# Moving an output product, sharing a division, writing a mask on another engine, and reordering the seam between two stages

## The reference, cut to what matters

```python
x = x + _L1_xattn_ref(_layernorm(x), ctx_1024, ctx_1024, mask_ik0, ...)    # 16 heads of 8, keys: 77
x = x + _L1_ffn_ref(_layernorm(x), ...)
x = x + _L2_xattn_ref(_layernorm(x), ctx_1024, ctx_1024, mask_fk1, ...)    # the same shape
x = x + _L2_ffn_ref(_layernorm(x), ...)      # 6 layers: windowed attention, then a gated FFN
x = x + _L3_xattn_ref(ctx_1024, _layernorm(x), mask_bk0, ...)              # 16 heads of 64, keys: 77 + 512
x = x + _L3_ffn_ref(x, ...)

def _L2_ffn_ref(...):                        # its last step, per layer
    xn = (x - mu) / jnp.sqrt(var + 1e-05) * g + bln
    a, gate = jnp.split(xn @ W1 + b1, 2, -1)
    return a * jax.nn.gelu(gate, approximate=False) @ W2 + b2

def _L3_xattn_ref(x, latents, mask, g1, b1, g2, b2, Wq, Wkv, Wout):
    xn, ln_lat = layer_norm(x, g1, b1), layer_norm(latents, g2, b2)
    q = ln_lat @ Wq
    k, v = jnp.split(jnp.concatenate([xn, ln_lat], axis=1) @ Wkv, 2, axis=-1)
    weight = jnp.einsum('bhld,bhnd->bhln', q * scale, k * scale)           # 512 x 589 per head
    weight = jnp.where(full_mask[:, None, None, :], weight, neg)           # only context keys are masked
    out = jnp.einsum('bhln,bhnd->bhld', softmax(weight), v)
    return out @ Wout
```

## Time and profile before

| | us |
|---|---|
| runs: median of 3 (lowest to highest) | 1956.83 (1955.41 to 1961.53) |
| the profiled execution, its own time | 1947.39 |
| its span, first to last instruction | 1945.5 |
| PE busy | 1621.7 (83%), mean granted clock 0.923 |
| DVE busy | 1255.0 (65%) |
| ACT busy | 968.0 (50%) |
| POOL busy | 761.1 (39%) |
| first attention, about | 230 to 301 |
| second attention, about | 484 to 555 |
| stack, about | 555 to 1480 |
| latents, about | 1490 to 1818 |

### The profile page before, as it was taken

One profiled execution on the slowest core, in us unless ns is written; L12 is line 12 of the kernel. 1 busy time (PEld: TensorE's weight loads), 2 busy tenths in 40 slices (PEclk: granted clock), 3 DMA queues, 4 the chain that ended last, 5 costly groups with the idle time before them and its releaser, 6 DMA issues.

```text
span 1945.5 us, 42200 instructions
## 1 busy us (share of the span) xinstructions
PE 1621.7 (83%) x17249; PEld 1097.3 (56%) x17249; DVE 1255.0 (65%) x2361; ACT 968.0 (50%) x1729; POOL 761.1 (39%) x1082
## 2 busy tenths in 40 slices
PE   3005576999767899989999889999987999999999
PEld 1002254676545666656666656666663677667576
DVE  6847684212866788868888778888853666666311
ACT  1034133332235567656666566666654666666332
POOL 0000020100247666766776657766740333334000
PEclk7556798899888999999999999999998999999999
DMA  3000002010033343433433343343311000000111
GB/s 108 20 4 0 3 1 62 22 33 14 1 113 98 98 117 102 124 81 105 118 103 102 101 102 101 117 109 89 96 35 43 2 1 1 1 2 1 33 33 33
DMA packets 73661, 113.33 MB, mean 58 GB/s; under 512 B 15942, under 2 KB 36012, under 8 KB 73438
## 3 DMA queue, kind: packets, MB, share of 16 engines
q1 hardware_dynamic: 72654, 110.40, 20.6%
q10 hardware_dynamic: 816, 0.24, 0.1%
HBM read 83.95 MB, written 27.50 MB: 57 GB/s over the span
## 4 chain that ended last, share of the span: by engine, by line
PE 60%; DVE 27%; issue 6%; ACT 4%; DVEq 1%; DMA 1%; POOL 0%; ACTq 0%; POOLq 0%; SPq 0%
PE PS L1385 7%; PE PS L1115 6%; PE PS L1106 6%; PE PS L2089 4%; PE PS L2043 3%; PE PS L1634 3%; PE PS L2068 3%; DVE st_t L1428 3%; DVE st_ss L1433 3%; PE PS L1514 2%; DVE st_r L1420 2%; PE PS L1493 2%; PE PS L1586 2%; PE PS L1733 2%; DVE al_hist L459 2%
## 5 line engine op out<-in xcount | busy, mean ns | idle before, releaser
L1462 POOL TENSOR_TENSOR st_r<-st_r,st_t 128x512 f32<-128x512 f32 x192 | 243.6, 1274 | 205.8 <-DVE st_t L1428 205.8
L1385 PE MATMUL PS<-st_wqkv,st_xs 128*128 128x512 f32 x576 | 304.8, 614 | 12.5 <-DVE st_t L1428 8.0
L2174 POOL TENSOR_SCALAR la_p<-la_p,la_rden 128x589 f32<-128x589 f32 x64 | 112.7, 1761 | 245.8 <-DVE la_rden L2193 245.8
L1479 POOL TENSOR_TENSOR st_r<-st_r,st_gy 128x512 f32<-128x512 f32 x192 | 195.1, 1047 | 3.8
L1420 DVE TENSOR_TENSOR st_r<-PS,st_rot 128x512 f32<-128x512 f32 x192 | 129.3, 673 | 99.0 <-ACT st_sqh L1404 98.4
L2187 DVE TENSOR_REDUCE la_nmx<-PS 128x1 f32<-128x589 f32 x128 | 92.7, 766 | 91.8 <-PE PS L2051 91.8
L2149 ACT ACTIVATE la_p<-PS,la_nmx 128x589 f32<-128x589 f32 x128 | 95.0, 747 | 106.6 <-DVE la_nmx L2187 106.6
L1174 ACT ACTIVATE m_h<-PS 128x512 f32<-128x512 f32 x128 | 76.1, 597 | 140.8 <-PE PS L1106 140.8
L1404 ACT ACTIVATE st_sqh<-PS 128x512 f32<-128x512 f32 x192 | 114.4, 596 | 57.4 <-PE PS L1385 56.3
L1199 DVE SCALAR_TENSOR_TENSOR m_y<-PS,m_g,m_y 128x128 f32<-128x128 f32 x112 | 31.5, 345 | 161.0 <-PE PS L1115 161.0
L1428 DVE TENSOR_TENSOR st_t<-PS,st_rot 128x512 f32<-128x512 f32 x192 | 130.6, 680 | 0.0
(11 more groups left out here) (313 smaller groups left out, 3487.4 us busy)
## 6 DMA issues: line engine op xcount, KB each, us to landing
st_v_out<-st_v SPq DMA_DIRECT2D x48, 512.0 KB, 2.6
st_vv<-st_v_out SPq DMA_DIRECT2D x96, 256.0 KB, 4.2
st_vv<-st_v_out SPq DMA_DIRECT2D x96, 192.0 KB, 4.5
st_wqkv<-in_st_wqkv SPq DMA_DIRECT2D x18, 512.0 KB, 5.7
m_w<-in_m_w SPq DMA_DIRECT2D x32, 256.0 KB, 3.1
st_vv<-st_v_out SPq DMA_DIRECT2D x72, 64.0 KB, 1.9
st_wo<-in_st_wo SPq DMA_DIRECT2D x6, 512.0 KB
st_w<-in_st_w SPq DMA_DIRECT2D x6, 341.0 KB
```

Source lines behind the costliest of these rows:

```text
L1385: pe.matmul(PS[:, 2 + m % 2, :], self.xs[:, b, P * t:P * t + P], self.wqkv[:, l % 2, k, 512 * half:512 * half + 512], start=True, stop=Tru ...
L1462: pool.tensor_tensor(r, r, self.t2[:, c % 2, :], ALU.add).then_inc(self.added, 1)
L1479: pool.tensor_tensor(r, r, y[:, 8 * c:8 * c + 8].unsqueeze(2).broadcast_to([P, 8, D2]), ALU.mult)\
L2174: pool.tensor_scalar(self.p[:, v % 2, 0, :], self.p[:, v % 2, 0, :], self.rden[:, v % 4, 0:1], None, ALU.mult).then_inc(self.scaled0, 1)
```

## The change

It has four parts.

1. **Attentions.** PE issues the output product of b=0 behind the scores of tile 6 (new `pe_out`, in step t=6) and no longer behind the mix of tile 3. ACT's copy to `l_o` now stands ahead of the exponential of that step. The division of the last tile is split (new `divide`): POOL takes heads 0 to 7, DVE heads 8 to 15, and PE's transposes wait for both.
2. **Stack, last unit.** The residual `xn` is added in `dve_xf`, for u=10 and u=11. The three chunks of u=11 use banks (6,7), (4,5), (0,1), so that no chunk waits for the one ahead of it, and `pe_down` waits chunk by chunk. Two table loads of ACT at the end are left out (the extra `ACT.Exp` ones).
3. **Seam.** The mean of b=0 is made right behind `pe_centre` of u=11, and its centring behind the last gate. The context pieces of latents (`ctx_pe`, `ctx_dve`) run ahead of `pe_down`. K and Q of b=0 start when b=0 is normed. V is made after them and waited for only in step v=1. The weights' transfers are issued when the stack's last projection is done.
4. **Latents.** The two mask products are gone. ACT writes the mask (128x77, bf16 in SBUF) into the PSUM columns of the context keys (`act_mask`), ahead of the scores, and the context product adds to it. The writes of v+1 stand in ACT's queue behind the copy L2162 of step v and ahead of the scaling L2168. The mask is prepared on 128 partitions.

```diff
                 pool.wait_ge(self.rden_ready, self.past["rden_ready"] + t + 1)
-                s = self.s[:, t % 3, 0:HK].rearrange("p (h k) -> p h k", h=H)
-                pool.tensor_tensor(s, s, self.rden[:, t % 2, :].unsqueeze(2).broadcast_to([P, H, KC]), ALU.mult)\
-                    .then_inc(self.probs, 1)
+                self.divide(pool, t, 0, H if t < NT - 1 else H // 2).then_inc(self.probs, 1)
+
+        def divide(self, eng, t, h0, h1):
+
+            s = self.s[:, t % 3, 0:HK].rearrange("p (h k) -> p h k", h=H)[:, h0:h1, :]
+            return eng.tensor_tensor(s, s, self.rden[:, t % 2, h0:h1].unsqueeze(2).broadcast_to([P, h1 - h0, KC]),
+                                     ALU.mult)
...
                                        kb[:, b, h0:h0 + nh, :].rearrange("p h k -> p (h k)"), start=True, stop=True)
                     mm.then_inc(self.scores, 1)
+                if t == NT // B + 2:
+                    self.pe_out(pe, 0)
                 if t >= 2:
                     u = t - 2
...
-                            pe.wait_ge(self.scores_read, self.past["scores_read"] + NT)
-                        pe.matmul(PS[:, 7 - 7 * b, :], self.wqo[:, 1, :], self.o[:, b, :], start=True, stop=True)\
-                          .then_inc(self.out_prod, 1)
+            pe.wait_ge(self.scores_read, self.past["scores_read"] + NT)
+            self.pe_out(pe, 1)
+
+        def pe_out(self, pe, b):
+
+            pe.wait_ge(self.o_ready, self.past["o_ready"] + b + 1)
+            pe.matmul(PS[:, 7 - 7 * b, :], self.wqo[:, 1, :], self.o[:, b, :], start=True, stop=True)\
+              .then_inc(self.out_prod, 1)
 
         def act(self, act):
...
                                        PS[:, 3 + g, 0:P * (c1 - c0)], ACT.Copy).then_inc(self.pT_ready, 1)
+                if t >= 2 and j == NT // B - 1:
+                    act.wait_ge(self.mixed, self.past["mixed"] + u + 1)
+                    act.activation(self.o[:, b, :], PS[:, 6, :], ACT.Copy).then_inc(self.o_ready, 1)
                 if t < NT:
                     act.wait_ge(self.centred, self.past["centred"] + t + 1)
                     s = self.s[:, t % 3, 0:HK]
                     act.activation(s, s, ACT.Exp).then_inc(self.exps, 1)
-                if t >= 2 and j == NT // B - 1:
-                    act.wait_ge(self.mixed, self.past["mixed"] + u + 1)
-                    act.activation(self.o[:, b, :], PS[:, 6, :], ACT.Copy).then_inc(self.o_ready, 1)
 
         def dve(self, dve):
...
                        .then_inc(self.centred, 1)
+            dve.wait_ge(self.rden_ready, self.past["rden_ready"] + NT)
...
+            latents.sp(sp)
 
...
+            if u // B == DEPTH - 1:
+
+                b = u % B
+                dve.wait_ge(self.xf_ready, u + 1)
+                order.link(dve, dve.tensor_tensor(x[:, b, :], x[:, b, :], xn[:, b, :], ALU.add))
...
+
+        def up_banks(self, u, j):
+            return ((6, 7), (4, 5), (0, 1))[j] if u == self.LAST else (6, 7)
+
         def pe_up(self, pe, u, j):
             l, (a, w) = u // B, self.CHUNKS[j]
+            gate, value = self.up_banks(u, j)
             if j == 0:
                 pe.wait_ge(self.ffn_in, u + 1)
                 pe.wait_ge(self.xu_ready, min(4 * u + 5, self.N))
-            else:
+            elif u < self.LAST:
                 pe.wait_ge(self.act_ready, 3 * u + j)
-            pe.matmul(PS[0:w, 6, :], self.w1[:, l % 2, FFI + a:FFI + a + w], self.xfn[:, :], start=True, stop=True)\
+            pe.matmul(PS[0:w, gate, :], self.w1[:, l % 2, FFI + a:FFI + a + w], self.xfn[:, :], start=True, stop=True)\
               .then_inc(self.up, 1)
-            pe.matmul(PS[0:w, 7, :], self.w1[:, l % 2, a:a + w], self.xfn[:, :], start=True, stop=True)\
+            pe.matmul(PS[0:w, value, :], self.w1[:, l % 2, a:a + w], self.xfn[:, :], start=True, stop=True)\
               .then_inc(self.up, 1)
 
         def act_gelu(self, act, u, j):
...
 
         def pe_down(self, pe, u):
             l = u // B
-            pe.wait_ge(self.act_ready, 3 * u + 3)
             for j, (a, w) in enumerate(self.CHUNKS):
+                if u == self.LAST or j == 0:
+                    pe.wait_ge(self.act_ready, 3 * u + (j + 1 if u == self.LAST else 3))
                 mm = pe.matmul(PS[:, 6, :], self.w2[0:w, l % 2, j, :], self.hid[0:w, j, :], start=(j == 0), stop=(j == 2))
             mm.then_inc(self.down, 1)
 
+        X_READY = 10
+
         def dve_down(self, dve, u):
             l, b = u // B, u % B
...
             dve.wait_ge(self.down, u + 1)
             dve.scalar_tensor_tensor(x[:, b, :], PS[:, 6, :], self.sv[:, l % 2, 2:3], x[:, b, :], ALU.add, ALU.add)\
-               .then_inc(self.down_added, 1)
-            dve.wait_ge(self.down_added, u + 1)
-            if u + B < B * DEPTH:
+               .then_inc(x_ready if final else self.down_added, 1)
+            if not final:
+                dve.wait_ge(self.down_added, u + 1)
                 self.shift(dve, b, self.xs[:, b, :], self.xs_ready)
 
...
                     self.pe_centre(pe, norm_of)
+                if norm_of == self.LAST:
...
                     self.pe_proj(pe, T + 2, 5)
+                if end_of == self.LAST:
+                    pe.wait_ge(self.act_ready, 3 * self.LAST + 1)
...
                     self.dve_gate(dve, end_of, 2)
-            for b in range(B):
-                dve.wait_ge(self.down_added, B * DEPTH)
-                dve.tensor_tensor(x[:, b, :], x[:, b, :], xn[:, b, :], ALU.add).then_inc(x_ready, 1)
+                if end_of == self.LAST:
...
 
         K0, K1, Q0, Q1, V0, V1, KCTX, VCTX = range(8)
         DVE_PIECES, ACT_PIECES = (K0, K1, KCTX, VCTX), (Q0, Q1, V0, V1)
-        FIRST_BANK = tuple(range(8))
+        FIRST_BANK = (0, 1, 2, 3, 6, 5, 7, 7)
+        FIRST = (KCTX, VCTX, K0, Q0, K1, Q1, V0, V1)
...
+        def ctx_pe(self, pe):
+
+            pe.wait_ge(align.cn_ready, 2)
+            pe.wait_ge(self.wc_in, self.c("wc_in", 16))
+            for k in (self.KCTX, self.VCTX):
+                self.pe_piece(pe, 0, k)
...
             for e in (1, 0):
-                pe.matmul(span[e][:, S:], q[e], self.k[rows[e], a, b, S:], start=True, stop=False,
-                          skip_group_check=True)
-            for e in (1, 0):
-                one = slice(D2 * e, D2 * e + 1)
-                pe.matmul(span[e][:, S:], oneb[one, :], mnegb[one, KC * b:KC * b + KC],
-                          start=False, stop=True, skip_group_check=True).then_inc(self.scores, 1)
+                pe.wait_ge(self.masked, 2 * v + 2 - e)
+                pe.matmul(span[e][:, S:], q[e], self.k[rows[e], a, b, S:], start=False, stop=True,
+                          skip_group_check=True).then_inc(self.scores, 1)
...
         def pe(self, pe):
-            norm.wait(pe, "pe")
-            pe.wait_ge(align.cn_ready, 2)
-            pe.wait_ge(self.wc_in, 16)
-            for k in range(self.PIECES):
-                self.pe_piece(pe, 0, k)
-            for k in range(self.PIECES):
+            for b, pieces in enumerate(((self.K0, self.Q0), (self.K1, self.Q1))):
+                norm.wait(pe, "pe", b + 1)
+                for k in pieces:
+                    self.pe_piece(pe, 0, k)
+            pe.wait_ge(*self.took(0, self.VCTX))
+            self.pe_piece(pe, 0, self.V0)
+            self.pe_piece(pe, 0, self.V1)
+            for k in (self.K0, self.Q0, self.K1, self.Q1, self.KCTX):
                 pe.wait_ge(*self.took(0, k))
             pe.wait_ge(self.w_in, self.c("w_in", 32))
             for v in range(self.STEPS):
                 self.pe_scores(pe, v)
+                if v == 1:
+                    for k in (self.V0, self.V1):
+                        pe.wait_ge(*self.took(0, k))
                 if v:
                     self.pe_turn(pe, v - 1)
...
             for k in self.ACT_PIECES:
                 self.act_piece(act, 0, k)
+                if k == self.Q1:
+                    act.wait_ge(*self.took(0, self.Q1))
+                    act.wait_ge(*self.took(0, self.K1))
+                    self.act_mask(act, 0)
...
+                if v + 1 < self.STEPS:
+                    self.act_mask(act, v + 1)
                 if v < self.STEPS:
                     self.act_scale(act, v)
+
+        def act_mask(self, act, v):
+
+            b = self.tile(v)[1]
+            if v:
+                act.wait_ge(self.exps, self.c("exps", 2 * v))
+            for e in (1, 0):
+                act.activation(self.span(e)[:, S:], mnegb[:, KC * b:KC * b + KC], ACT.Copy).then_inc(self.masked, 1)
```

130 lines of the change are left out of this document (73 added, 57 removed).

## The result

The changed kernel takes 1930.70 us, the median of 4 runs (1927.56 to 1934.96), against 1956.12 before: a ratio of 0.9865, with a 95% interval of 0.9835 to 0.9894. The gain of the medians is 25.4 us, and the interval reaches from 21 to 32; the forecast was 29.0. In a second comparison the same two kernels gave a ratio of 0.9856 (0.9834 to 0.9878), 24 to 33 us. Over the ten runs of both the changed kernel's median is 1930.7.

What follows compares the result with a forecast made beforehand. DVE was taken to bound the attentions, a chain of short steps the seam, and PE latents. 14.7 - 0.3 + 6.5 + 8.1 = 29.0 us off the median 1956.8 gave 1927.8, range 1920 to 1938.

Steps and rivals of the forecast that it cites:

- Attentions, 14.7: Both attentions: DVE's waits at tile 6 close, 7.5 and 6.7 us, and split last divisions give 0.3 and 0.2.
- Division: Last division of each attention: POOL's and DVE's halves go one after the other, 2.0 for 2.25; gains 0.3 and 0.2.
- Stack, -0.3: Stack, u=10: DVE's residual addition can wait for one of POOL's scalings; loss 0.3 us, bounds 0 and 1.7.
- Seam, 6.5: Last unit's first chunk to latents' first scores: six terms, -0.2 + 2.5 + 0.7 + 0.9 + 1.2 + 1.4, gain 6.5 us.
- Banks and chunks: Seam: chunks 1 and 2 run without a round trip over ACT and DVE, so the down product starts 2.5 us earlier.
- one more group gives 2 less: Seam: if one more group of four passes falls in PE's low clock, the seam gives 2 us less.
- Latents, 8.1: Latents' loop: without mask products 56 of 64 steps give 0.14 us each, 7.8, plus 0.3 for start and end.
- They delay the scaling L2168, which PE's transposes of head 1 need: Latents: two mask writes, about 0.5 us, delay this scaling; slack 1.08 mid-loop covers it, 0.28 in the last eight steps.
- cost the gain of latents' loop: Rival in latents: slow writes or smaller slack make transposes wait in every step; 1936 us, chance 0.12.
- close a loop over ACT: Rival in latents: writes, scores and exponentials wait on each other, 32 us lost instead of 8 gained; 1968 us, chance 0.03.
- From 0.6 us a write on: Latents: the length of one ACT mask write from which the loop gives nothing.
- The holes didn't fill otherwise: Rival in the attentions: PE is late with transposes in the next tile, DVE stalls 3 us in each; 1934, chance 0.03.

Runs made afterwards that it cites:

- the first profile: The profiled execution of the changed kernel in its first measurement, nothing edited; span 1929.1 us, and the median of those runs 1930.70 us.
- the second profile: The profiled execution, 1922.85 us, when the changed kernel was run once more with nothing edited; median of those runs 1929.73 us.
- the experiment: Changed kernel, but the last unit's three chunks share banks 6 and 7 again and the context pieces stand behind the last gate; 1934.84 us.
- masks_twice: Changed kernel with two more 128x77 writes by ACT in each of latents' steps, going to a spare SBUF tile; 1936.17 us.

## Why the prediction was right, point by point

The forecast was 1927.8, the measured medians 1930.7 and 1929.7, and 1920 to 1938 held them. The mechanisms of the attentions and the seam held, and latents' loop gained by the one named, though one of its steps failed. The stack's small loss had another cause than the one named, and that the stack's start came within 0.1 of the attentions' term is luck. By its own terms:

- **Attentions, 14.7.** Holes 7.5 and 6.7, measured 7.6 and 6.8. Division 0.3 and 0.2, measured 0.4 and 0 in the first profile (the transposes stood behind a slow mix), and 0.4 and 0.7 in the second profile, where the transposes come right behind the division in both attentions (1.93 from its start, against 2.30 and 2.67 before). The stack starts 14.8 earlier, two shifts of 1.9 in untouched work having cancelled. That the halves go one after the other was read from the timeline of before and is in POOL's 1.83 beside DVE's 0.80. The Trainium skill, page "SBUF — State Buffer", section "SBUF: two separate sides", has it as an exclusive lock for the whole instruction; the trace agrees: 0.80 and 1.03 are 1.83.
- **Stack, -0.3.** Measured -0.15 in four profiles and -0.9 in the first. The named mechanism, waiting for POOL's scaling, did not occur in those four: the addition took its 0.69 there and started before the scalings did. It occurred in three profiles in which a long pause of PE came before (1.41 in each, and in the first the shift was caught as well, so that DVE was about 2.2 later).
- **Seam, 6.5.** Measured 6.0 from the centring product to the first scores (38.32 before, 32.37 after). The mean of b=0 cost nothing, the stretch even got 0.4 shorter (forecast -0.2). Banks and chunks 2.8 (2.5), shown alone by the experiment: 3.4 with the context pieces uncovered. Residual and half the norm 1.5 (1.6). The start of K and Q 0.7 (1.2), since the spreading ran at half clock. Pieces and copies 1.5 (1.4). And one cost that the sum had only in its range: one more product pair of K and Q fell in the low clock, -0.9. The prediction's "one more group gives 2 less" was for four products' passes; half such a group fell in and cost half of it, so the price was right.
- **Latents, 8.1.** Measured 6.84. The step that failed is "They delay the scaling L2168, which PE's transposes of head 1 need": they also delay the copy of the projection piece behind it, which the transposes need as well, and it had less slack. Six of eight steps give 0.13 to 0.14, the fifth gives 0.04 and the seventh 0.06: 0.19 less in eight, 1.3 in seven groups. The price of a write, 0.26, was 0.244. Two smaller errors about cancel: four of the last seven steps did give 0.14, 0.5 in all, where the prediction counted none (the other three gave nothing, for the reason it named), and the 0.3 for the start and the end is not in the loop. The gain is shown in the loop only; the kernel with the products on PE again was no slower as a whole.
- **Rivals.** The writes neither cost the gain of latents' loop (it is 6.8 slower with the mask products) nor close a loop over ACT (two more writes: 7.2 in 288, not 26). "From 0.6 us a write on" the loop gives nothing was too high: with four writes, 0.8 together, as two of 0.4 would take, the gain was gone. The slack had been read at one of eight kinds of steps, and at one of two instructions. The holes didn't fill otherwise, but only because both orders were changed.

Sum of what was measured: 14.8 + 6.0 + 6.8, less 0.15 to 0.9 for the stack, is 26.7 to 27.4, against 29.0. It fits the two comparisons (21 to 32, and 24 to 33). They are too wide to say how much of latents' 6.8 reaches the whole kernel, which the mask products' run leaves in doubt.

**Why the pair of profiles shows 16.4.** Of the 12.6 us missing, 1.7 are the terms just told (latents 1.3, seam 0.5, attentions -0.1), and 0.6 is the addition in the stack, beyond the 0.3. The other 10.3 are 6.0 in the stack (eleven pauses of 34.1 us against ten of 29.2, and low clock behind them) and 4.3 in the last experts at low clock. They are events of an execution, since other profiles of the same program lack them: the profile of before had lain 9.4 under the median of its runs, that of the changed kernel lay on its own. The prediction took the 9.4 off alike, so its 1927.8 didn't hang on it, but its 1918.4 for a profiled execution did.

## What to carry to other kernels

When a slack is read from a loop, read it at every kind of step that the loop has, and for every instruction that stands behind the added one in its queue: here it was 1.08 in the step that was read and nothing in another. When two engines hand a buffer round, move both ends: each half of the attentions' reorder alone left a wait of 1.6 to 3.4 us. In a kernel whose executions scatter by 13 us, judge a change of 7 by the stretch that it touches, where that repeats within 0.2, and not by a pair of whole profiles. And when a loss is put down to an edit, first take off how late the engine already was: of the 1.1 to 1.3 us that seemed to be the addition's, 0.15 were.

## What the runs showed of the hardware that was not expected

**PE pauses in the middle of a run of products.** Timeline of the changed kernel, PE alone; 128 products L1530 of one tile break off after 100:

```profile
1381.34 1.19 PE L1530 MATMUL PS<-st_kT,st_qT 64*32 64x64 f32 x100
1385.26 0.45 PE L1530 MATMUL PS<-st_kT,st_qT 64*32 64x64 f32 x28 [2.73 <-issue]
```

The DMA view of 1380 to 1386 (busy share in 40 slices, then the queues):

```profile
DMA  8989999999999799954200000000000000000000
...
q1 hardware_dynamic: 331, 0.58, 46.7%
q8 instruction: 1, 0.02, 1.4%
```

The 16 engines are full of data from 1380 to about 1382.6 and all but idle from 1383 on, so most of the pause has no data beside it. One packet of the instruction queue (q8) is in these 6 us, between 1382.3 and 1382.5. The queue has 137 packets and 2.24 MB over the span, 16 KB each. No wait on a semaphore is shown, and the places hardly move between kernels, as they would for an instruction stream that is fetched in pieces.

The packet's time is what ties the two together. The eleven pauses of the first profile, with the time at which PE goes on and that of the last packet of this queue ahead of it (within 0.1, from the DMA view):

```
PE goes on    596.75  616.06  636.33  656.50  819.97  859.48 1072.98 1092.77 1115.12 1330.50 1385.26
packet         594.1   613.5   634.0   653.9   817.5   856.8  1070.3  1090.2  1112.8  1328.1  1382.4
```

PE goes on 2.3 to 2.9 us after a packet each time, though in this stretch one comes only every 4 to 14 us, and so it does in ten pauses of other profiles, three of them the short ones of 0.8 to 1.1 us. In masks_twice, whose last layer has no pause of over 0.5 us, a packet passes at 1374.4 with the DMA engines idle and another at 1370.4 with them full; so a packet beside full engines does not always make a pause. That the instructions come late behind data is inferred from this and from the shorter pauses without loads; no run took the instruction queue away. Eight to eleven pauses make 23 to 34 us of a kernel of 1930.

The Trainium skill, page "Runtime: NRT & Kernel Launch", section "Instruction fetch mechanics", says that instructions come in blocks of 16 KiB through a DMA queue of the sequencer's own, and that crossing from one block to the next is mostly hidden. The packets' size agrees; at eight to eleven places of this kernel it is not hidden.

**The clock behind short waits.** From the start of K and Q to V it took 5.1 to 6.6 us in ten profiles, with products of 1.9 us (granted clock 0.53 over the 6.6 us of the first profile), and 3.54 in the three kernels in which products filled PE's waits ahead (granted clock 1.00 in the first of them). In two other norms the same filling showed nothing: ahead of the stack the products stayed at 5.37 us, and ahead of the last experts 7.11 us at full clock also occurs without it.
